# Decoder kernel on one core: fillers, weight turns, token turns and weight product in a new order, and the context squares as one two-part row per batch

## The reference

```python
def _L0_attn_ref(x, Wk, Wq, Wv):
    K = x @ Wk
    Q = x @ Wq
    V = x @ Wv
    scores = jnp.einsum('bnd,bmd->bnm', Q, K) / jnp.sqrt(jnp.float32(d))
    ...
    attn = jax.nn.softmax(scores, axis=-1)
    return attn @ V
...
        def _pairwise_euclidean(a, b):
            aa = jnp.sum(a * a, axis=-1)[:, None]
            bb = jnp.sum(b * b, axis=-1)[None, :]
            ab = a @ b.T
            return jnp.sqrt(jnp.maximum(aa + bb - 2.0 * ab, 0.0))
...
    x = x + _L0_attn_ref(_layernorm(x, axis=-1), L0_attn_Wk, L0_attn_Wq, L0_attn_Wv)
    x = x + _L0_xattn_ref(ctx_1024, _layernorm(x, axis=-1))
```

## Time and profile before

| | |
|---|---|
| median of 3 runs | 613.42 us |
| all runs | 612.35, 613.42, 632.77 us |
| the profiled execution, its own time | 615.58 us |
| its span, from the first to the last instruction | 613.8 us |
| mean granted TensorE clock | 0.869 |
| busy: TensorE, weight loads, VectorE, ScalarE, GpSimd | 464.3, 361.5, 356.8, 193.7, 167.1 us |
| chain that ended last, by engine | TensorE 55%, VectorE 18%, DMA 7%, ScalarE 6% |

### The profile page before, as it was taken

The page is one execution under the profiler, slowest core; times in us unless marked ns, Lnnn a source line. Parts: engine busy times, 40 slices in busy tenths (PEclk is TensorE's granted clock), DMA queues, the critical chain, the costliest instruction groups (busy, mean ns, idle before and its releaser), DMA issues.

```text
span 613.8 us, 8989 instructions
## 1 busy us (share of the span) xinstructions
PE 464.3 (76%) x2915; PEld 361.5 (59%) x2915; DVE 356.8 (58%) x1216; ACT 193.7 (32%) x471; POOL 167.1 (27%) x247
## 2 busy tenths in 40 slices
PE   4999997000004877899999988799987998799980
PEld 4786466000004867677777877677764675688750
DVE  4586597996899757353222266656743356444454
ACT  2376532000014241123222022665724352055400
POOL 5124002100000030544632225322106020365253
PEclk9999999555555996999999989958998996799995
DMA  9502476951004863210320130220037001155634
GB/s 218 109 1 69 84 44 40 168 87 33 2 3 132 299 202 99 60 52 27 95 60 29 55 107 0 62 86 2 3 111 226 1 1 60 35 152 159 127 91 115
DMA packets 58109, 50.76 MB, mean 83 GB/s; under 512 B 23238, under 2 KB 51208, under 8 KB 57840
## 3 DMA queue, kind: packets, MB, share of 16 engines
q1 hardware_dynamic: 46592, 34.62, 22.8%
q0 software_dynamic: 6992, 14.80, 10.1%
q10 hardware_dynamic: 4480, 0.76, 1.0%
HBM read 37.62 MB, written 10.84 MB: 79 GB/s over the span
## 4 chain that ended last, share of the span: by engine, by line
PE 55%; DVE 18%; DMA 7%; ACT 6%; issue 5%; POOL 4%; SPq 4%; ACTq 1%; POOLq 0%; DVEq 0%
PE ps L1166 45%; PE ps L1169 11%; DVE big L1801 4%; SPq L623 3%; POOL big L907 2%; DMA big<-skew 2%; DVE mtmp L1797 2%; DVE big L1816 2%; ACT big L1090 1%; ACT N_r L945 1%; ACT big L925 1%; DVE big L1835 1%; DVE big L1836 1%; DMA big<-in_L_attn_wo 1%; DMA big<-in_L_attn_Wk 1%
## 5 line engine op out<-in xcount | busy, mean ns | idle before, releaser
L1166 PE MATMUL ps<-big,ctxT_r 128*128 x368 | 109.2, 429 | 0.3 <-ACT ctxT_r L925 0.3
L1169 PE MATMUL ps<-ident,big 128*128 128x128 f32 (+5 forms) x410 | 63.2, 290 | 14.5 <-DMA big<-in_L_attn_Wk 8.0
L1166 PEld LDWEIGHTS ps<-big,ctxT_r 128*128 128x128 f32 x368 | 64.5, 190 | 15.4 <-issue 10.6
L1166 PE MATMUL ps<-ones,esel 8*112 8x1 f32 x2 | 0.5, 332 | 88.7 <-DVE esel L1851 88.7
L1169 PEld LDWEIGHTS ps<-ident,big 128*128 128x128 f32 (+5 forms) x410 | 50.1, 153 | 29.4 <-issue 16.8
L925 ACT ACTIVATE big<-ps 128x512 f32<-128x512 f32 (+5 forms) x55 | 34.4, 652 | 90.0 <-PE ps L1166 48.1
L925 ACT ACTIVATE ctxT_r<-ps 128x256 f32<-128x256 f32 (+3 forms) x74 | 30.6, 440 | 77.0 <-PE ps L1169 67.4
L1166 PEld LDWEIGHTS ps<-ones,esel 8*112 8x112 f32 x2 | 0.4, 282 | 89.1 <-DVE esel L1851 89.1
L1166 PE MATMUL ps<-big 112*32 112x112 f32 (+4 forms) x698 | 45.8, 314 | 4.7 <-ACT big L1090 2.1
L1166 PE MATMUL ps<-ident 128*128 128x128 f32 (+1 forms) x374 | 49.2, 294 | 0.0
L1166 PEld LDWEIGHTS ps<-ident 128*128 128x128 f32 x374 | 48.1, 211 | 0.1
(11 more groups left out here) (257 smaller groups left out, 922.1 us busy)
## 6 DMA issues: line engine op xcount, KB each, us to landing
big<-in_L_ffn_W SPq DMA_DIRECT2D x16, 512.0 KB, 8.1
routed<-Vc_r SPq DMA_DIRECT2D x29, 128.0 KB, 2.3
ctxT_r<-in_ctx POOLq DMA_DIRECT2D x4, 750.0 KB, 18.1
big<-in_ctx SPq DMA_DIRECT2D x4, 672.0 KB
big<-in_L_ffn_Wg SPq DMA_DIRECT2D x16, 128.0 KB, 2.5
big<-in_L_ffn_Wu SPq DMA_DIRECT2D x16, 128.0 KB, 2.5
big<-in_L_ffn_Wd SPq DMA_DIRECT2D x16, 128.0 KB, 2.5
normed<-N_r SPq DMA_DIRECT2D x2, 896.0 KB, 5.1
```

What stands on the lines that cost most here:

```text
L1166: return nc.tensor.matmul(dst, lhsT, rhs, start=first, stop=last)
L1169: return nc.tensor.transpose(dst, src, ident[0:n, 0:n])
```

## The change

TensorE starts with twelve fillers before it waits for the weights (`WARM_START`); the two groups of six are gone. The token turns of the first half now stand before the product of the weights, and ScalarE's copies follow that order. VectorE takes statistics of two pairs and then norms both. After the last context square VectorE makes four small things: a row that sums two blocks of the identity, a column of zeros, the first part of -aa/2 rounded to the split type, and the remainder as a second part. TensorE turns both parts in three turns of 16 rows into one row of 375 columns per batch and part, and a single product of 16 rows by 376 columns in the split type adds them for a batch.

```diff
@@ -185,8 +185,12 @@
         spill = big[0:CR, o_sq:o_sq + 2 * D].rearrange("p (a n) -> p a n", a=2)
-        ctx_sq = big[0:CR, o_sq + 2 * D:o_sq + 2 * D + NCH]
-        ctx_sqT = big[0:NCH, o_sq + 2 * D + NCH:o_sq + 2 * D + NCH + CR]
+        (o_sum, o_part, o_turned, o_one) = place(o_sq + 2 * D, NCH, 2 * NCH, S + 1, B)
+        assert o_one + B <= o_rb
+        ctx_sq = big[0:CR, o_sum:o_part].rearrange("p (c b) -> p c b", c=CH)
+        sq_part_s, sq_part = (t[0:CR, o_part:o_turned].rearrange("p (c a b) -> p c a b", c=CH, a=2) for t in (big_s, big))
+        ctx_sqT = big_s[0:2 * B, o_turned:o_one]
+        one_row = big_s[0:2 * B, o_one:o_one + B]
@@ -353,7 +357,8 @@
-        WARM = ((6, 0), (0, 0), (0, 0), (60, 0), (0, 0), (6, 2))
+        WARM_START = 12
+        WARM = ((0, 0), (0, 0), (0, 0), (60, 0), (0, 0), (6, 2))
@@ -361,8 +366,8 @@
         r_wt0 = ring.take(act, act)
+        ln_slots[0] = ring.take(act, act)
         (r_wqk,) = ring.take(act)
-        ln_slots[0] = ring.take(act, act)
@@ -952,8 +957,8 @@
             for w, slot in enumerate(r_wt0):
                 copy(slot, wT0[:, w], bank(slot)[:, :].rearrange("p (k n) -> p k n", k=KD))
+            ln_turned(0, halves=(0,))
             copy(r_wqk, wqk, bank(r_wqk)[:, :].rearrange("p (k n) -> p k n", k=KD))
-            ln_turned(0, halves=(0,))
@@ -974,7 +979,7 @@
-            copy(r_aa, ctx_sqT, bank(r_aa)[0:NCH, 0:CR], ACT.Identity, scale=-0.5)
+            copy(r_aa, ctx_sqT[:, 0:S], bank(r_aa)[0:2 * B, 0:S])
@@ -1218,6 +1223,7 @@
             pe.wait_ge(s["ident_ready"], 1)
+            keep_warm(r_wt0[0], WARM_START)
             pe.wait_ge(s["w0_loaded"], 32)
@@ -1225,15 +1231,14 @@
-            keep_warm(r_wqk, WARM[0][0])
+            ln_turn(0, (0,))
             wait_act(r_wt0[1])
-            dst = ps[:, r_wqk.bank, :]
+            dst = bank(r_wqk)
...
-            ln_turn(0, (0,))
@@ -1258,7 +1263,7 @@
-            wait_act(ln_slots[0][KD - 1])
+            wait_act(r_wqk)
             queries(0)
@@ -1276,8 +1281,7 @@
             def context_squares(b, dst):
 
-                for c in range(CH):
-                    mm(dst[0:T, c * CR:(c + 1) * CR], view(ident, CH * b + c, [[0, T]], (0, NCH)), ctx_sqT, c == 0, False)
+                mm(ps[0:T, r_dist[b].bank, 0:S + 1], bass.AP(one_row.tensor, one_row.offset + b, [one_row.ap[0], [0, T]]), ctx_sqT, True, False)
@@ -1299,8 +1303,11 @@
-            pe.wait_ge(s["ctx_sq_ready"], NCH)
-            filled(turn(bank(r_aa)[0:NCH, 0:CR], ctx_sq, CR))
+            pe.wait_ge(s["sq_parted"], 4)
+            dst = bank(r_aa)
+            for c in range(CH):
+                last = turn(dst[0:2 * B, c * CR:(c + 1) * CR], sq_part[:, c].rearrange("p a b -> p (a b)"), CR)
+            filled(last)
@@ -1717,8 +1724,11 @@
-            for q4 in range(B // 2):
-                ln_step(0, q4, lambda b: ve.wait_ge(s[f"x_loaded{b // HB}"], 16))
+            for h in range(2):
+                for q4 in (2 * h, 2 * h + 1):
+                    ln_stats(0, q4, lambda b: ve.wait_ge(s[f"x_loaded{b // HB}"], 16))
+                for q4 in (2 * h, 2 * h + 1):
+                    ln_norm(0, q4)
@@ -1726,7 +1736,7 @@
-                                           accum_out=ctx_sq[:, j:j + 1]).then_inc(s["ctx_sq_ready"], 1)
+                                           accum_out=ctx_sq[:, j % CH, j // CH:j // CH + 1]).then_inc(s["ctx_sq_ready"], 1)
@@ -1740,6 +1750,14 @@
+            ve.wait_ge(s["ident_ready"], 1)
+            v.tensor_tensor(one_row, ident[0:2 * B, 0:B], ident[0:2 * B, B:2 * B], ALU.add).then_inc(s["sq_parted"], 1)
+            v.tensor_scalar(ctx_sqT[:, S:S + 1], ident[0:2 * B, 0:1], 0.0, None, ALU.mult).then_inc(s["sq_parted"], 1)
+            ve.wait_ge(s["ctx_sq_ready"], NCH)
+            v.tensor_scalar(sq_part_s[:, :, 0], ctx_sq, -0.5, None, ALU.mult).then_inc(s["sq_parted"], 1)
+            ve.wait_ge(s["sq_parted"], 3)
+            v.scalar_tensor_tensor(sq_part_s[:, :, 1], ctx_sq, -0.5, sq_part_s[:, :, 0], ALU.mult, ALU.subtract)\
+                .then_inc(s["sq_parted"], 1)
             for i, slot in enumerate(r_pt0):
```

More of the change, by code:

```diff
@@ L517, in decoder_kernel @@
                  "norm_hi_ready", "aux_loaded", "stats_ready", "rstd_ready", "norm_ready",
-                 "p0_exp", "s0_ready", "bb_ready", "ctx_sq_ready", "pad_ready", "pad_stored", "costs_clear", "row_found",
+                 "p0_exp", "s0_ready", "bb_ready", "ctx_sq_ready", "sq_parted", "pad_ready", "pad_stored", "costs_clear", "row_found",
                  "column_marked", "inv_ready", "dist_ready",
```

## The result

| | before | after |
|---|---|---|
| median in the comparison | 618.36 us of 4 runs | 620.78 us of 4 runs |
| runs | 612.35, 613.42, 623.29, 632.77 | 616.47, 618.98, 622.58, 627.34 |
| profiled execution: own time, span, mean granted clock | 615.58, 613.8, 0.869 | 627.34, 624.7, 0.838 |

The ratio is 1.0128, with a 95% interval of 1.0071 to 1.0186: within 2%, and on the slower side. Ratios in this text compare, of each kernel, only executions within 1.5% of its fastest, which leaves 612.35 and 613.42 before and all but 627.34 after. The prediction said 607.2, with a range of 603.0 to 610.5.

A forecast was written before the change was run, and what follows sets the result against it. Key weights' landing, TensorE, the last distance store, then SyncE's queued loads were taken to bound the kernel, the rest following by semaphores. Terms 4.65 + 1.6 = 6.25 off 613.42 gave 607.2 us, range 603.0 to 610.5.

The forecast's parts named there:

- Term 1: Opening on TensorE: fillers off the path and token turns before the weights' product bring first queries at 12.45, minus 4.65 us.
- rival A: Opening: clock not up at 8 us, so turns and product run slow; 2.0 us lost, 609.2; chance 0.15.
- Term 2: Distance stage: squares as rows shorten TensorE's pairs, SyncE then binds, last store goes at 66.7 against 68.37, minus 1.6 us.
- The 2.7 us a pair: SyncE's distance stores: alternative from the skill's 2.0 us fixed part plus 0.63 for loads; SyncE would not bind, term minus 2.3.
- After the store ... they start that much earlier: SyncE's loads after the last distance store: same packets and order, 33 us, starting earlier by what the store gains.
- the rest of the kernel changed, which I hold for unlikely: Sign for the whole kernel: what both terms right and a median off by more than 3 would say.
- Rival D: Slow stretch around 405 us changes length: shorter gives 599 to 603, longer by 6 gives 610; chance 0.10, half each side.
- Rival C: Queries, scores and values: clock stays low throughout, adds 17 us, kernel ends at 624; chance 0.03.

The follow-up runs named there:

- early fillers: 24 more fillers on TensorE before it waits for the path's first input: changed kernel 609.22 us, repeated 606.15; kernel before 616.81; opening alone 612.55.
- fourth group: Changed kernel unchanged, twice: 611.52 and 614.05 us; kernel before unchanged: 614.29; changed kernel with 24 fillers ahead of the path and 7 after it: 604.38.

## Why the prediction was wrong

**Term 1, the opening: right.** Queries 4.65 earlier in the forecast; the profile shows 5.3, and the means over six traces with the old opening (16.8) and nine of the changed kernel with its opening (12.0) 4.8. The one trace with late weights is rival A and cost what A said. That the other ten escaped it was in part luck. The prediction took a gap as harmless by one row, the idle 1.83 us ahead of the 36 passes of the expansion at 7.99. Of ten traces with that same idle time seven have 7.99 to 8.00 and three, those of three versions with early fillers, 9.63, 9.68 and 10.82. In the first profile the weights came when the fillers ended, and there was no gap to pass.

**Term 2, the rows: right in mechanism, a little small.** From first queries to last store the old squares take 51.3 us in every trace and the new ones 49.1 (once 49.4), which is 2.2 and not 1.6. SyncE did become the bound with 3.45 a pair; the slip was the first pair, which I had held to come 0.4 later by ScalarE's longer copy and which came 0.2 earlier (first query to first store 38.66 us against 38.88). The 2.7 us a pair that the prediction worked out beside it did not come: SyncE took 3.45. It had taken from the Trainium skill (DMA: Bandwidth & Descriptors, Anatomy of one DMA) the fixed part of about 2.0 us alone, where the section, written for transfers that GpSimd issues, adds a part by the bytes; for a store of 329 KB both together give an estimate of 2.75 us, and the row has 2.73.

**"After the store ... they start that much earlier": right in the mean, not in one trace.** From last store to the 49th column the traces have 34.6 to 38.6 us, so a single pair of profiles shows the column 3.3 to 8.7 us earlier, depending on the pair. The path's start is at 192.2 before (mean of 5 traces with this opening and these squares) and at 184.6 after (mean of 9), 7.7 earlier before rounding, where 6.25 were summed. The terms as measured, 4.8 and 2.2, give 7.0; the rest is within this spread.

**The step that failed** is the sentence that everything after the column loop follows by semaphores, together with "the rest of the kernel changed, which I hold for unlikely". The prediction put the change of everything behind the path's start at nothing. The stage of the path has two lengths, 19 or 31 us, by whether the granted clock rises in it, and in the traces of the two kernels as they are the expansion takes 8.0 behind the short one and 10.6 to 10.9 behind the long one. I read only the stages that the diff touches and two rows on the clock elsewhere. The price could have been worked out from the profile: 14 fillers of 64 columns take 1.69 us at the full clock, so near 3.4 at half of it (3.12 was measured), more than VectorE's step of 2.08. Rival D named a slow stretch that changes, at 405 us, with plus 6 at most and 5% on the slow side. That stretch did grow, by some 1.5 us against the profile of before, but the main loss was at 188: it costs 12 in the stage and 3 behind it, and by the mean clock it was there in 19 of 42 executions of the changed kernel. Rival C had the right mechanism, a clock that stays low under a busy TensorE, in the wrong place.

**The base.** The prediction stood on 613.42, the median of three runs. Over 122 executions of the kernel before that came with the experiments the median is 616.3, and 32 of them (26%) have a mean clock below 0.864. These have a median of 625.6, the others 614.6.

**What the change is worth.** Over 42 executions of the changed kernel, the first four among them: median 612.1. Those with a mean clock from 0.857 up, 23, have 607.6, which is 7.0 less than the like of before, and the 19 others 622.6. So the forecast time of 607.2 is near the median of a little more than half of the executions, and not that of the kernel; the first comparison had none of them. That 607.6 lies so near 607.2 is in part luck: the base was 1.2 us too low for executions of this kind and the gain 0.8 too small.

**Still open: does the change make the low clock likelier?** 19 of 42 against 32 of 122 would be p = 0.03 by Fisher's test, but it is 15 of 38 without the four that raised the question, p = 0.15, and p = 0.07 when these 38 are compared group by group with the 75 executions of before beside them (both sides of the test counted). In the group counted with limits fixed beforehand it was 5 of 12 against 1 of 17 (p = 0.06); equal odds had let expect 3 or 4 of 12. The limits are weak too: 0.864 for the kernel before was chosen from its runs, whose clocks run on without a gap there (0.862, 0.863, 0.864, 0.865). If the odds are those of the kernel before, the changed one's median would be near 609 to 610; if two in five, near 611 (estimates from its 42 executions). No trace shows a cause for other odds: TensorE has no work in either kernel in the 88 us ahead of the path. So it is shown what a low execution loses, and not why an execution is low.

The Trainium skill (TensorE: Matmul & The Clock Gate, Part 1) warns that the point of the rise varies from run to run, that clock events in a trace are unreliable, that the clock has been seen stuck at a quarter for more than 50 us, and that the ramp is under 1% of a typical kernel. The traces agree with the first. They show it stuck as well, though at 0.50 and for 36 us. Here the durations (3.12 against 1.69 us for the same 14 passes) confirm the recorded clock. The last is not so here: 12 to 15 us of 610.

## What to carry to other kernels

Products that nobody reads, issued to keep the clock up, are work like any other when it is down: size them so that a step still fits under its partner engine at the slow rate, or start them while the engine would idle anyway, ahead of the stage and not in it. Here 24 of them ahead of the path left no low execution of the changed kernel (0 of 18 against 19 of 42), and one of 12 of the kernel before. When a kernel's runs spread over 3%, look at the mean clock of each run before you compare medians, and check whether the change merely met another mix of executions; four runs can all be of one kind.

## What the runs showed of the hardware

- After 88 us of idle TensorE, the same instruction sequence raises the clock 3.7 to 4.7 us after its start in six traces and not within the stage in four, in which TensorE was busy for 29 us from there and the granted clock 0.50. Which it is differs from run to run of one program on one chip (traces at 601.39 and 616.59 us of the changed kernel, fourth group).
- In these four traces and in the one without the twelve passes of 128 columns ahead of the steps, the step's fillers (passes of 64 columns) and turns ran at the lower level for 25 us and more without a rise. It came 4.9 to 6.1 us into the expansion's passes of 256 columns, at 221.4 in the first profile. Without those twelve passes all four executions have a mean clock of 0.857 or less.
- An idle time of 1.3 to 1.5 us after the opening's fillers left the next eight turns at 1.09 us; 2.27 us made them 1.97. An idle time of 1.83 us ahead of the expansion left its 36 passes at 7.99 to 8.00 in seven traces and made them 9.63 to 10.82 in three.
